# The loop over steps 3 to 6 of a dense convolution block, written out on every engine

## The chip, the cores and the metric

The kernel runs on one core of one Trainium2 chip. The metric is the device time of that core in microseconds (us), as the median of several executions. A profiled execution gives in addition a page and a trace; its span is measured from the first to the last instruction.

## What is computed

Two blocks follow each other on a float32 image batch `x` of 16 x 32 x 32 x 32 (images, channels, rows, columns). The first:

```python
x1 = relu(conv2d(x, w1, b1, 2, 2))
x2 = relu(conv2d(concatenate((x, x1), 1), w2, b2, 2, 2))
x3 = relu(conv2d(concatenate((x, x1, x2), 1), w3, b3, 2, 2))
x4 = relu(conv2d(concatenate((x, x1, x2, x3), 1), w4, b4, 2, 2))
fea = relu(concatenate((x, x1, x2, x3, x4), 1))
fea = einsum('ij,bcjk,lk->bcil', H, fea, H)
out = conv2d(fea, w6, b6, 1, 1) + x
```

Each `conv2d` is a 3x3 convolution; the first four are dilated by 2. The second block quantises its input and its weights to four bits, with one scale for each tensor, and computes

```python
out = relu(_qconv(x, w1))
out = relu(_qconv(out, w2, stride=1, padding=1, groups=PLANES))
out = _qconv(out, w3)
return out + x
```

Since a scale needs the maximum over the whole tensor, the second block starts when the first is done for all images.

## The kernel before

`dense_block` computes the first block, two images (u = 0 and 1) a step. Steps 0 to 7 each convolve one pair; the transform with H and the last convolution ("mix", `stage1`, `stage3`) of a pair lag behind, so that step s also mixes pair s - 1, and step 8 only finishes. Every engine has its own `step(s, odd, batch)`, a hand-written order of work, and all engines run it through `steps` (line 151 and after): 0, 1 and 2 are written out, 3 to 6 stand as a loop of two passes with two steps in each, 7 and 8 are written out. In the loop the step's number is a register, so every wait whose count depends on it (`pe.wait_ge(halo_in[2][u], (s + 1) * 32)` and its like) has the count worked out on the engine's sequencer first, or compares with a register that is counted up.

Engines meet at semaphores alone. What matters below is one step of TensorE (PE), in its order:

- `conv0` and `conv0_on` (line 768), 36 matmuls on x of both images;
- `mix(p, 0)` (lines 871 and 875);
- `conv1_alone` (line 827) and `conv1` (line 768), which end what x2 needs;
- `stage3` of the pair before (line 909), 1.0 us;
- `conv2(s, 0)` and `conv2(s, 1)` (line 768, 9 matmuls each), which read tile `D2`, the split x2, with its halo rows. They wait for `halo_in[2][u]`;
- `mix(p, 1)`, `conv3` (line 827) and `stage1` (line 900).

A halo is made of DMAs that copy 32 partitions of `D` to other partitions of `D`, shifted by a row: `halos` on SyncE (SP), lines 219 and 222, and for `D2` of image 0 one of the two on ScalarE's queue (`halo_2`, line 354). They start when VectorE (DVE) has split x2 (`split_2`, line 490), which follows `conv1_alone` by two additions (lines 499 and 505). So in each step the way from `conv1_alone` over DVE and the DMAs to `conv2` runs beside `conv1` and `stage3` on PE.

SP also issues in each step the loads of x for the next pair (line 212), of x for the mix (229), of the residual (289), and the gathers of the features into `F` (239). The second block, `quantised_block`, has loops of its own on PE, DVE and ACT (lines 1258, 1061, 1070, 1140, 1195).

Of the kernel before, what the change touches and what calls it, by code (L numbers as in the profile page):

```python
# [77 lines left out]
def dense_block(nc, block, semaphore, x_res, x_pads, x_mix, w_conv, bias, w_mix, h_cols, h_rows, b6, w_int, ident_in, keep):  # L78
# [7 lines left out]
    with ExitStack() as ctx:  # L86
# [65 lines left out]
        def steps(eng, step):  # L152
            step(0, 0, -1)
            step(1, 1, 0)
            step(2, 0, 0)
            with eng.Fori(0, 2) as k:
                step(k * 2 + 3, 1, k + 1)
                step(k * 2 + 4, 0, k + 1)
            step(7, 1, 3)
            step(8, 0, 3)  # L160
# [48 lines left out]
        def _(sp):  # L209
# [44 lines left out]
            def step(s, odd, batch):  # L254
# [34 lines left out]
                sp.dma_start(xb[odd][:].rearrange("p u n -> p (u n)"), x_res[s]).then_inc(xb_in[odd], 16)  # L289

            steps(sp, step)

        @block.gpsimd
# [22 lines left out]
        def _(act):  # L316
# [102 lines left out]
            def step(s, odd, batch):  # L419
# [37 lines left out]
                if not is_before_last(s):  # L457
                    copy_4(1)

            steps(act, step)  # L460

            act.wait_ge(sum_done, 2 * PAIRS - 2)
# [9 lines left out]
        def _(dve):  # L472
# [202 lines left out]
            def step(s, odd, batch):  # L675
# [79 lines left out]
                low_4(s, 1)  # L755

            steps(dve, step)

        @block.tensor
# [743 lines left out]
```

## Time and profile before

| what | value |
|---|---|
| median of 3 runs | 394.29 us (392.97 to 395.1) |
| profiled execution, its own time | 394.38 us |
| span of the profiled execution | 392.6 us |
| PE busy | 370.5 us, 94% of the span |
| DVE, ACT busy | 289.0 us, 234.6 us |
| granted TensorE clock, mean | 0.986 |

The profile's page gives busy times of each engine, their course over the span in 40 slices, the DMA queues, the chain of work that ended last and the costliest groups of instructions. PEld is the loading of weights, which overlaps the matmuls.
A row of a stretch gives its bounds and length, the busy time of PE, PEld, DVE, ACT and POOL with their numbers of instructions, the granted clock, the mean share of the DMA engines and GB/s. A row of a timeline gives start, length, engine, line and what was done, and in brackets the idle time before it and what ended it; a row of the chain gives start, length and what. A row of a DMA queue gives its number and kind, packets, MB and share of the stretch on 16 engines; a row of DMA issues gives what was moved by which queue, how often, KB each, and the time from issue to landing.

The trace gives the same for stretches: in the profiled execution step 2 runs on PE from 66.40 to 101.87 us, step 3 to 137.59, step 4 to 174.57, step 5 to 210.05, step 6 to 245.52, and step 7's last stage follows from about 281 us on. The loop's back edge is therefore at 174.57 on PE, its entry at 101.87 and its exit at 245.52.

### The profile page before, as it was taken

The numbers are of one execution on the slowest core, as the hardware profiler recorded it, in microseconds if no ns is written. First come the engines' busy times: TensorE is split into PE (matmuls) and PEld (weight loads), VectorE is DVE, ScalarE is ACT, GpSimd is POOL, SyncE is SP. The second block draws the span as 40 slices with busy tenths as digits, with TensorE's granted clock in tenths as the row PEclk, the third lists the DMA queues.
The fourth block names the chain that finished last, engine by engine and source line by source line (L and its number), as shares of the span: only waits on it lengthen the run. The fifth ranks groups of instructions, "written<-read, shape, count | busy, mean of one in ns | idle before, by whom it ended". The sixth has DMA issues, their size and how long they took to land.

```text
span 392.6 us, 8020 instructions
## 1 busy us (share of the span) xinstructions
PE 370.5 (94%) x2870; PEld 270.8 (69%) x2873; DVE 289.0 (74%) x545; ACT 234.6 (60%) x377; POOL 13.5 (3%) x17
## 2 busy tenths in 40 slices
PE   8989999999999999899999999999984897999986
PEld 7867876878687788668786877887663342455532
DVE  5867678558937984696589379846986699677876
ACT  5446659537743955395367449544846696287761
POOL 6000000300030000000000000000000000000000
PEclk9999999999999999999999999999997699999999
DMA  8847254315333622453253334224100000000004
GB/s 242 237 100 189 66 119 142 93 45 131 100 80 89 173 61 53 100 144 93 48 120 104 79 86 113 60 55 112 55 2 2 1 0 0 3 2 2 4 27 187
DMA packets 19533, 32.56 MB, mean 83 GB/s; under 512 B 4528, under 2 KB 11568, under 8 KB 19504
## 3 DMA queue, kind: packets, MB, share of 16 engines
q1 hardware_dynamic: 18864, 31.14, 30.4%
q10 hardware_dynamic: 640, 1.03, 1.2%
q8 instruction: 18, 0.29, 0.3%
q14 instruction: 11, 0.09, 0.1%
HBM read 11.38 MB, written 2.10 MB: 34 GB/s over the span
## 4 chain that ended last, share of the span: by engine, by line
PE 78%; DVE 11%; DMA 4%; issue 3%; ACT 2%; DVEq 0%; ACTq 0%
PE sums_ps L768 28%; PE mix_ps L871 12%; PE ps L1307 7%; PE mix_ps L900 5%; PE mix_ps L827 5%; PE sums_ps L827 5%; PE mix_ps L875 4%; DMA D<-D 4%; PE ps L1347 3%; PE ps L1274 2%; DVE part L499 2%; PE mix_ps L909 1%; PE ps L1271 1%; PE mix_ps L811 1%; DVE q_I L1190 1%
## 5 line engine op out<-in xcount | busy, mean ns | idle before, releaser
L768 PE MATMUL sums_ps<-D,w_hl 128*128 128x512 f32 x504 | 122.9, 399 | 2.0 <-DMA D<-D 2.0
L768 PEld LDWEIGHTS sums_ps<-D,w_hl 128*128 128x128 f32 x504 | 93.5, 188 | 32.2 <-issue 6.3
L871 PE MATMUL mix_ps<-mix_hl,F_hl 128*128 128x288 f32 x360 | 64.4, 296 | 0.5 <-ACT Y L390 0.5
L390 ACT ACTIVATE Y<-mix_ps 128x288 f32<-128x288 f32 x120 | 48.9, 410 | 24.1 <-PE mix_ps L875 12.2
L871 PEld LDWEIGHTS mix_ps<-mix_hl,F_hl 128*128 128x128 f32 x360 | 55.4, 190 | 2.8 <-ACT Y L390 1.2
L328 ACT ACTIVATE r<-sums_ps,bias_sb 64x512 f32<-64x512 f32 x28 | 19.1, 682 | 48.2 <-PE sums_ps L768 48.1
L499 DVE TENSOR_TENSOR part<-mix_ps,part 64x512 f32<-64x512 f32 x16 | 11.1, 693 | 38.9 <-PE mix_ps L827 38.4
L1073 ACT ACTIVATE q_I<-ps,w_bias 128x1024 f32 x24 | 25.4, 1110 | 16.6 <-PE ps L1307 16.6
L875 PE MATMUL mix_ps<-mix_hl,X 96*128 96x288 f32 x120 | 35.3, 298 | 0.0
L1307 PE MATMUL ps<-q_q,diag 64*64 64x512 bf16 x576 | 33.3, 389 | 0.4 <-DVE q_q L1168 0.4
L348 ACT ACTIVATE D<-part 64x512 fp32r<-64x512 f32 x16 | 10.7, 670 | 32.6 <-DVE part L505 32.6
L1307 PEld LDWEIGHTS ps<-q_q,diag 64*64 64x64 bf16 x576 | 19.2, 105 | 14.5 <-issue 0.9
L900 PE MATMUL mix_ps<-Y,hc 32*32 32x512 f32 (+1 forms) x576 | 24.4, 567 | 0.6 <-ACT Y L390 0.6
L827 PE MATMUL mix_ps<-D,w_hl 128*128 128x512 f32 x96 | 23.9, 397 | 0.0
L827 PE MATMUL sums_ps<-D,w_hl 128*128 128x512 f32 x96 | 23.7, 396 | 0.0
L481 DVE CAST D<-r 64x512 fp32r<-64x512 f32 x32 | 13.4, 419 | 14.0 <-ACT r L328 13.3
L564 DVE SCALAR_TENSOR_TENSOR values<-St,b_sb,xb 64x128 f32<-64x128 f32 (+1 forms) x64 | 22.2, 346 | 0.9
L483 DVE TENSOR_TENSOR D<-r,D 64x512 fp32r<-64x512 f32 x32 | 21.9, 684 | 1.1
L875 PEld LDWEIGHTS mix_ps<-mix_hl,X 96*128 96x128 f32 x120 | 22.5, 189 | 0.0
L531 DVE SCALAR_TENSOR_TENSOR X<-part,X 32x512 fp32r<-32x512 f32 x32 | 21.8, 681 | 0.7
L1274 PE MATMUL ps<-q_xq,w_q 128*128 128x386 bf16 x72 | 21.0, 355 | 0.2 <-ACT q_I L1067 0.2
L522 DVE SCALAR_TENSOR_TENSOR F_hl<-F,F_hl 128x1024 fp32r<-128x1024 f32 x16 | 19.5, 1217 | 2.1 <-ACT F_hl L364 1.8
(133 smaller groups left out, 510.6 us busy)
## 6 DMA issues: line engine op xcount, KB each, us to landing
D<-D SPq DMA_DIRECT2D x88, 126.0 KB, 2.3
x_own<-in_x_pads SPq DMA_DIRECT2D x16, 288.0 KB, 3.7
F<-r SPq DMA_DIRECT2D x64, 64.0 KB, 2.0
F<-in_x_mix SPq DMA_DIRECT2D x16, 128.0 KB, 2.4
F<-part SPq DMA_DIRECT2D x32, 64.0 KB, 2.0
xb<-in_x_res SPq DMA_DIRECT2D x8, 256.0 KB, 2.7
out<-q_res SPq DMA_DIRECT2D x8, 256.0 KB, 2.0
w_raw<-in_w_conv SPq DMA_DIRECT2D x6, 192.0 KB, 4.4
```

The costliest lines, as they stand in the source:

```text
L390: nc.scalar.activation(Y[:, u, g], banks(p, u)[:, g % 4, 0:MIX], ACT.Copy).then_inc(y_out, 1)
L483: nc.vector.tensor_tensor(out=own(f, u, 1), in0=src, in1=high.bitcast(F32), op=ALU.subtract).then_inc(own_ready[u], 1)
L531: last = nc.vector.scalar_tensor_tensor(out=X4[u][low, h], in0=part[u][k].rearrange("p a b l -> p (a b l)"), scalar=0.0, in1=X4[u][k, h].b ...
L564: last = nc.vector.scalar_tensor_tensor(out=keep.values[64 * pi:64 * pi + 64, batch, m, PH // 2 * a:PH // 2 * (a + 1), :], in0=st[k, pi], ...
L768: last = nc.tensor.matmul(conv_sums(s, u)[:, bank, :], w_hl[:, wp, n, d, :], D[f][u][:, xp, :, 4 * d:4 * d + RUN], start=start and d == 0 ...
L827: last = nc.tensor.matmul(side_sums(s, u, f), w_hl[:, w, n, d, :], D[f - 1][u][:, x, :, 4 * d:4 * d + RUN], start=d == 0 and w == 0, stop= ...
L871: nc.tensor.matmul(y, F_hl[u][:, xp, h, k], mix_hl[:, wp], start=n == 0, stop=False, skip_group_check=True)
L875: nc.tensor.matmul(banks(p, u)[:, g % 4, 0:MIX], X4[u][:, g // 4, NP * (g % 4):NP * (g % 4) + NP], mix4_hl[:], start=False, stop=True, ski ...
L900: last = nc.tensor.matmul(out[32 * dy:32 * dy + 32, j, 0:PX // 4 * len(us)], hc[k, d], y, start=d == 0, stop=d == 2, skip_group_check=True)
L1073: nc.scalar.activation(I[:, g, b, 0:PX], ps[:, 2 * b:2 * b + 2].rearrange("p k n -> p (k n)"), ACT.Relu, bias=keep.w2_bias[:, bass.ts(g, 1 ...
L1274: last = nc.tensor.matmul(c1_slot(ps, j)[:, h], w_q[:, bass.ts(k * 2 + par, NP)], x_low[:, at:at + CUT], start=j not in C1_OFFSET, stop=True)
L1307: last = nc.tensor.matmul(ps[64 * col:64 * col + 64, 2 * (two + b) + h], diag[rows, g, at:at + 2].rearrange("p q c -> p (q c)"), field[:, ...
```

## The change

The loop becomes a Python loop that is run when the program is built: each engine's code for steps 3 to 6 then stands twice as long, `s` is a number in all of it, and the functions that ask for it (`is_first`, `no_next` and the like) answer as before. Nothing else is touched. The four loops of the second block stay.

```diff
             step(0, 0, -1)
             step(1, 1, 0)
             step(2, 0, 0)
-            with eng.Fori(0, 2) as k:
+            for k in range(2):
                 step(k * 2 + 3, 1, k + 1)
                 step(k * 2 + 4, 0, k + 1)
             step(7, 1, 3)
```

PE, middle of step 3, from the end of `mix(p, 0)` to the start of `mix(p, 1)`, before (`D` are the convolutions' inputs, `Zt` the transform's):

```order
L875 MATMUL mix_ps<-mix_hl,X 128x288
L833 REGISTER_ALU
L835 ISA
L827 MATMUL mix_ps<-D,w_hl 128x512 x6
L835 REGISTER_ALU
L827 MATMUL mix_ps<-D,w_hl 128x512 x6
L768 MATMUL sums_ps<-D,w_hl 128x512 x18
L968 REGISTER_ALU
L906 ISA
L909 MATMUL mix_ps<-Zt,hr 32x256 x4
L906 REGISTER_ALU
L909 MATMUL mix_ps<-Zt,hr 32x256 x4
```

The same place of the changed kernel:

```order
L875 MATMUL mix_ps<-mix_hl,X 128x288
L827 MATMUL mix_ps<-D,w_hl 128x512 x12
L768 MATMUL sums_ps<-D,w_hl 128x512 x18
L909 MATMUL mix_ps<-Zt,hr 32x256 x8
L768 MATMUL sums_ps<-D,w_hl 128x512 x18
```

The matmuls stand in the same order; the six register instructions between them are gone. Over a pass of two steps PE's waits and register instructions together are 48 before and 20 now (counted in the two built programs).

SP, from the end of step 2 into step 3, before:

```order
L289 DMA xb<-in_x_res 128x512 [waits mx_done]
L156 UNCONDITIONAL_BRANCH
L156 ISA
L212 ISA [waits x_split1,x_split0]
L212 DMA x_own<-in_x_pads 128x576
L212 ISA
L212 DMA x_own<-in_x_pads 128x576
L229 ISA [waits f_lo0]
L229 DMA F<-in_x_mix 32x1024
L236 REGISTER_ALU
L239 DMA F<-r 32x512 [waits relu_done0]
```

and of the changed kernel:

```order
L289 DMA xb<-in_x_res 128x512 [waits mx_done]
L212 DMA x_own<-in_x_pads 128x576 [waits x_split1,x_split0]
L212 DMA x_own<-in_x_pads 128x576
L229 DMA F<-in_x_mix 32x1024 [waits f_lo0]
L239 DMA F<-r 32x512 [waits relu_done0]
```

The transfers and their waits stand in the same order; the registers that held addresses and counts are gone.

## Rows read from the trace of the kernel before

**Rows 1.** The profile's page: span, PE's busy time, chain by engine

```profile
span 392.6 us, 8020 instructions
...
PE 370.5 (94%) x2870; PEld 270.8 (69%) x2873; DVE 289.0 (74%) x545; ACT 234.6 (60%) x377; POOL 13.5 (3%) x17
...
PE 78%; DVE 11%; DMA 4%; issue 3%; ACT 2%; DVEq 0%; ACTq 0%
```

**Rows 2.** Stretches: steps 2 to 6, busy time of each engine

```profile
66.40:101.87 35.47, 35.47 (x249) 28.11 (x249) 25.93 (x46) 21.36 (x39) 3.04 (x3) 1.00 0.39 98
101.87:137.59 35.72, 35.72 (x249) 28.12 (x249) 25.96 (x46) 21.33 (x39) 3.04 (x3) 1.00 0.39 98
137.59:174.57 36.98, 35.56 (x249) 28.20 (x249) 25.87 (x46) 21.33 (x39) 0.95 (x2) 1.00 0.38 95
174.57:210.05 35.48, 35.48 (x250) 28.18 (x249) 25.90 (x46) 21.37 (x39) 0.00 (x0) 1.00 0.38 97
210.05:245.52 35.47, 35.47 (x249) 28.17 (x249) 25.89 (x46) 21.32 (x39) 0.00 (x0) 1.00 0.34 81
```

**Rows 3.** Timeline of PEld at the starts of steps 4 and 5

```profile
137.51 0.53 PEld L768 LDWEIGHTS sums_ps<-D,w_hl 128*128 128x128 f32 x3 [0.84 <-issue]
...
174.50 0.53 PEld L768 LDWEIGHTS sums_ps<-D,w_hl 128*128 128x128 f32 x3 [0.84 <-issue]
```

**Rows 4.** The chain (start, length, what) at `conv2` of steps 3, 4 and 5

```profile
122.74 4.62 PE sums_ps L768 x18
...
154.83 5.00 DMA D<-D
...
195.44 4.39 PE sums_ps L768 x18
```

**Rows 5.** PE's timeline at `conv2` of steps 4 and 7

```profile
159.88 1.66 PE L768 MATMUL sums_ps<-D,w_hl 128*128 128x512 f32 x6 [1.42 <-DMA D<-D]
...
266.58 2.12 PE L768 MATMUL sums_ps<-D,w_hl 128*128 128x512 f32 x8 [0.19 <-DMA D<-D]
```

**Rows 6.** DMA queues: whole span; steps 3; 4; packets of 5 and 6

```profile
q8 instruction: 18, 0.29, 0.3%
...
q8 instruction: 3, 0.05, 0.7%
...
q8 instruction: 2, 0.03, 0.4%
...
DMA packets 3843, 6.32 MB, mean 89 GB/s; under 512 B 897, under 2 KB 2433, under 8 KB 3843
```

**Rows 7.** DMA queues of 86.2:86.3, 121.7:121.9, 157.2:157.3, 263.7:263.8

```profile
q8 instruction: 1, 0.02, 54.9%
...
q8 instruction: 1, 0.02, 32.3%
...
q8 instruction: 1, 0.02, 59.9%
...
q8 instruction: 1, 0.02, 79.2%
```

**Rows 8.** DMA issues at 119.1, 154.8, 191.8, 262.8: halo of image 0

```profile
D<-D ACTq DMA_DIRECT2D x1, 126.0 KB, 3.1
...
D<-D ACTq DMA_DIRECT2D x1, 126.0 KB, 5.0
...
D<-D ACTq DMA_DIRECT2D x1, 126.0 KB, 2.9
...
D<-D ACTq DMA_DIRECT2D x1, 126.0 KB, 3.7
```

**Rows 9.** Timeline of SP: second halo DMA of image 1, steps 3 to 5

```profile
122.17 1.03 SPq L222 DMA_DIRECT2D D<-D  x1
...
157.65 0.89 SPq L222 DMA_DIRECT2D D<-D  x1
...
194.69 0.60 SPq L222 DMA_DIRECT2D D<-D  x1
```

## The prediction

> **What bounds the kernel now.** I read the page first, then the span cut into steps, then what stands at the loop's edges, then the few waits of TensorE (PE) that are left in the loop. On the page PE is busy 94% of 392.6 us and makes 78% of the chain that ended last [rows 1]. Cut into steps, the picture is sharper: in step 2, which is written out, PE is busy for all of its 35.47 us, and in step 6, which is the last quarter of the loop's work, for all of its 35.47 us too; step 5 takes 35.48, step 3 35.72 and step 4 36.98 [rows 2]. DVE and ACT are busy 26 and 21 us of each [rows 2]. So these steps are PE's, back to back, and whatever is done by a sequencer beside them is covered. The one thing to find is why steps 3 and 4 are longer than their twins 5 and 6, which run the same code: 0.25 and 1.50 us. The chain and PE's timeline answer: in step 4 the matmuls of `conv2` wait 1.42 us for the halo of `D2` [rows 5], a DMA issued at 154.83 that took 5.00 us [rows 4]. In step 3 `conv2` is 4.62 us long instead of 4.39 as in step 5 [rows 4], a small wait between its two images. In step 7 the same wait is 0.19 us [rows 5].
>
> The DMA rows then show what those places have in common. The twin halo takes 2.9 us in step 5, 3.1 in step 3, 3.7 in step 7 and 5.0 in step 4 [rows 8]. The engines' code arrives in 16 KB packets (18 of them are 0.29 MB) on an instruction queue, 3 in step 3 and 2 in step 4, while in steps 5 and 6 together all 3843 packets are under 8 KB, so none is of this kind [rows 6]: the second pass finds its code in place. And one of these packets starts at 86.2, 121.7, 157.2 and 263.7 us, which is 19.8, 19.9, 19.6 and 18.2 us into steps 2, 3, 4 and 7 [rows 7], in the middle of the halos that `conv2` waits for. 59.9% of 0.1 us on 16 engines is 0.96 us, the time that this one packet holds one DMA engine; the others come to 0.88, 1.03 and 1.27 us [rows 7]. I take it that a halo is spread over the DMA engines and lands when the slowest is done; then one engine held for 1 us can delay all of it. SP is touched as well: its issue of the last halo DMA takes 0.60 us in step 5, 1.03 and 0.89 in steps 3 and 4 [rows 9].
>
> **Part 1: the branches and the loop register.** Entry, back edge and exit on PE, DVE, ACT and SP go. What they cost is read at PE's back edge, the only place where they could lengthen the step: before the first weight load of step 5, behind the back edge, the loader idles 0.84 us, and before that of step 4, in the middle of the loop's body with no branch, 0.84 us as well [rows 3]. PE works on the last transform's matmuls meanwhile. On DVE and ACT a branch stands in 35 us of which 9 and 14 are idle [rows 2]. Gain: 0. Above, it is bounded by the difference of steps 5 and 2, 0.01 us.
>
> **Part 2: the counts in registers.** 28 instructions of PE's sequencer in two steps go, and more on ACT and DVE. Step 2 has constants everywhere, step 6 registers everywhere; both take 35.47 us, with the same 28.1 us of weight loads and the same DVE and ACT time within 0.05 us [rows 2]. Gain on the path: 0. The cover here is PE's backlog of matmuls; where PE waits for others, as in the way from `conv1_alone` to `conv2`, the register instructions are done before the semaphore arrives. If none of this held, the gain would still be under the 0.01 us just read.
>
> **Part 3: the code gets longer.** This is the one part that can move the time, and it goes both ways. In the built programs PE has 4,763 instructions before and 5,745 after, with matmul and weight load as two and the float32 matmuls of the transform doubled as in the trace. 18 packets for 4,763 are about 260 each, so I take 256 a packet, and 982 more instructions are 4 more packets: two in step 5 and two in step 6, where there is none now. A step is 249 matmuls and 249 loads [rows 2] and, with constants, some 10 waits: about 506 to 508 instructions, 4 to 6 under two packets. So every step has one fetch in its middle and one at its end, and the middle one slips later by that much from step to step; in the loop of before the extra registers (14 a step) made it slip earlier, which is why step 4's comes 0.3 us sooner than step 3's. Between a fetch in step 3 that cost 0.25 us and one in step 4 that cost 1.50 us lie these 0.3 us [rows 2, 7].
>
> Now place them. Half a step's 14 register instructions less puts step 3's fetch some 10 instructions later, step 4's some 23, step 5's and 6's a further 6 each. PE passes 36 instructions (18 matmuls) in 4.4 us of convolution, and 32 in the 1.0 us of `stage3`, which lies just there, so an estimate is 20.1 us into step 3, 20.2 into step 4, 20.3 to 20.5 into step 5, 20.9 into step 6 and 21.9 into step 7, each give or take 0.5. Image 0's halo is issued 17.2 us into a step (154.83 less 137.59) and takes 2.9 undisturbed [rows 4, 8], so it is down at 20.1 and these fetches come too late to hold it: step 4's 1.42 us [rows 5] should go. Image 1's second DMA is issued 20.1 us into step 5 (194.69 less 174.57) [rows 9]; from the same row it is late by 0.3 to 0.4 us if a fetch is under way, and its conv2 half starts 2.2 us after the first, at 23.1. Step 3 is the nearest row for what this is worth: 0.25 us. A fetch deeper in this transfer can cost more; the ends are 0 (step 2's fetch at 19.8 cost nothing, 35.47 us) and 1.5 (step 4's) for each [rows 2, 7]. I take 0.25 for steps 3, 4 and 5 and 0.5 for steps 6 and 7, where the estimate falls deepest into image 1's transfer.
>
> The sum, in waits of PE on the halo: before, 0.25 + 1.50 + 0 + 0 + 0.2 = 1.95 us. After, 0.25 + 0.25 + 0.25 + 0.5 + 0.5 = 1.75. Difference -0.2 us. Against the profiled execution, 394.38 us (span 392.6 and 1.8 around it), this gives 394.2; that execution lies 0.1 above the median of the three runs, 394.29, so I forecast **394.1 us**.
>
> The other engines' code grows too, by one small packet or so each on ACT, DVE and SP; the nearest price is the same wait, and these are half as long. I cost them at nothing and keep up to 0.5 us in the range. The second block's loops stay and only lie at other addresses.
>
> A rule speaks of this change. The Trainium skill, "Runtime: NRT & Kernel Launch", section "Instruction fetch mechanics", says that a taken branch whose target is not in the window of loaded pages stalls for a fetch, and that kernels therefore prefer to be unrolled. The same section gives PE 128 KiB, 2048 instructions, which the body of some 1,040 fits into. By the rule's first half each back edge would be worth a fetch; the trace does not agree, since step 5 starts after the same 0.84 us as step 4 and no packet comes in.
>
> **The rivals.**
>
> *All collisions gone* (faster). If the later fetches miss the halos altogether, as step 2's did, steps 3 to 7 are all 35.47 us and 1.95 us go: 394.3 - 1.95 = 392.4. For it: step 2. Against it: SP's issue of the last halo DMA was slow in both loop steps that had a fetch [rows 9], and the fetches of steps 6 and 7 slip into the transfer.
>
> *The fetches hit two more halos hard* (slower). Steps 5 and 6 have no code fetch now and take 35.48 and 35.47 [rows 2]. If the fetch there falls as unluckily as in step 4, each costs 1.5 us, and if step 4's stays, the time is 394.3 + 3.0 = 397.3. It decides where the fetch starts while more than half of a halo's transfer is still to come. For it: the only fetch that came a little early cost 1.5. Against it: the code's length moves them later, not earlier, and image 1 has more slack, 0.7 us.
>
> *The branch did stall an engine* (faster). If entry and back edge each hid a fetch of about 1 us on DVE or ACT that held up PE later, 2 us would go: 392.3. Against it: no longer step stands behind either edge [rows 2].
>
> *Nothing moves at all* (same): the fetch of step 4 hits as before and steps 5 and 6 get 0.25 each: 394.8.
>
> **How the numbers follow.** Forecast 394.1 with a chance of 0.60; nothing moves, 394.8, 0.17; all gone 392.4, 0.11; hit hard 397.3, 0.09; a hidden stall 392.3, 0.03. About 0.5%, 2.0 us, is what a measurement of this kernel can tell from no change: bounds 392.3 and 396.3. The forecast's own spread is the bounds of five waits of 0 to 1.5 us that hardly all fall one way, 393.0 to 395.6. The range leaves out hard hits and the far side of the clean cases: 392.4 to 396.2. Faster by over 0.5%: half of the clean case and of the stall, 0.07. Slower: 0.09 and a little of the forecast's tail less the milder hits, 0.09. Same: 0.84.
>
> **What would show it.** Right, part 1 and 2: steps 2 and 5 or 6 equal where no halo is late, the loader's 0.84 us unchanged. Part 3: 22 packets of 16 KB instead of 18, two of them in each of steps 5 and 6, the middle one 20 to 21 us in; step 4 at 35.7 us instead of 36.98; PE's waits inside steps 3 to 7 all on `D<-D`; ACT's halo DMA at 2.9 to 3.1 us in step 4. Wrong: a step that is shorter than 35.47 us, which would mean that registers or branches did cost PE time; a wait of over 1 us in step 5 or 6, which is the slower rival; a new wait on something other than a halo.

## The result: 0.7% slower

| kernel | median | executions | profiled span |
|---|---|---|---|
| before | 394.05 us (392.57 to 395.11) | 19 | 392.6 us |
| loop written out | 396.79 us (395.41 to 398.39) | 19 | 394.1 us |

The ratio is 1.0069, with a 95% interval of 1.0055 to 1.0082: a loss of 2.7 us. Here and below, times are medians of several executions, and step lengths and rows come from the one profiled execution of each kernel. The forecast was 394.1 us in a range of 392.4 to 396.2, so the time lies above the range.

The page of the changed kernel, to be laid beside [rows 1, 6]: span, busy time by engine, instruction queue, chain by engine.

```profile
span 394.1 us, 7685 instructions
...
PE 371.2 (94%) x2873; PEld 270.0 (69%) x2873; DVE 288.7 (73%) x545; ACT 234.5 (60%) x377; POOL 13.5 (3%) x17
...
q8 instruction: 22, 0.36, 0.4%
...
PE 73%; DVE 14%; DMA 6%; issue 3%; ACT 2%; SPq 1%; DVEq 0%; ACTq 0%
```

PE is as busy as before, and DVE and ACT too. What changed is the chain: 5% of the span, about 20 us, has gone from PE to DVE, DMA and SP. The instruction queue has the 22 packets that were forecast instead of 18.

The changed kernel cut into steps 2 to 7, as in [rows 2] (bounds and length, then busy times and counts):

```profile
65.51:101.03 35.52, 35.52 (x250) 28.09 (x249) 25.93 (x46) 21.35 (x39) 3.04 (x3) 1.00 0.38 98
101.03:137.65 36.62, 35.74 (x250) 28.09 (x249) 25.90 (x46) 21.36 (x39) 3.04 (x3) 1.00 0.38 96
137.65:174.25 36.60, 35.73 (x249) 28.08 (x249) 25.89 (x46) 21.34 (x39) 0.95 (x2) 1.00 0.37 95
174.25:211.20 36.95, 35.74 (x250) 28.11 (x249) 25.91 (x46) 21.35 (x39) 0.00 (x0) 1.00 0.38 95
211.20:247.41 36.21, 35.74 (x249) 28.11 (x249) 25.90 (x46) 21.36 (x39) 0.00 (x0) 1.00 0.32 80
247.41:282.88 35.47, 35.47 (x249) 28.16 (x249) 24.54 (x44) 20.21 (x37) 0.00 (x0) 1.00 0.33 78
```

Each of the four steps of the old loop is now 0.7 to 1.5 us over the 35.47 us that a step takes when nothing is late. Steps 3 to 6 sum to 146.38 us against 143.65 before [rows 2]: 2.73 us more. Step 7 gives 0.26 back, because its wait is gone, and step 2 loses 0.05, so that steps 2 to 7 are 2.5 us longer, near the 2.7 of the medians. In the two profiled spans only 1.5 us are seen, above all because this execution of the changed kernel reached step 2 0.89 us earlier (65.51 against 66.40). That seems to be a chance of the start, for both kernels run the same code up to there: by their timelines the 18 passes of the first convolution took 4.48 us here and 5.12 before, and the wait for a DMA at 22 us is 1.42 here and 1.61 before.

The chain through the middle of step 5 (start, length, what):

```profile
187.12 1.42 PE mix_ps L827 x6
...
191.57 0.69 DVE part L505
...
192.28 0.67 ACT D L348
...
193.76 0.59 SPq L219
...
194.39 4.18 DMA D<-D
```

It runs from `conv1_alone` over DVE, ACT and SP's issue of image 1's halo into its second DMA, 4.18 us long. PE's timeline at the end of that halo in steps 3 and 5:

```profile
125.06 2.14 PE L768 MATMUL sums_ps<-D,w_hl 128*128 128x512 f32 x8 [0.88 <-DMA D<-D]
...
198.62 0.73 PE L768 MATMUL sums_ps<-D,w_hl 128*128 128x512 f32 x2 [1.21 <-DMA D<-D]
```

The wait stands between the two images of `conv2`, not in front of the first as in step 4 before [rows 5]. And the packets are there: instruction queue from 195.6 to 195.7 us, then the landings of image 1's halo DMAs issued at 194.3 and 231.3, from the list of DMA issues:

```profile
q8 instruction: 1, 0.02, 103.8%
```

```profile
D<-D SPq DMA_DIRECT2D x2, 126.0 KB, 3.3
...
D<-D SPq DMA_DIRECT2D x1, 126.0 KB, 3.4
```

103.8% of 0.1 us on 16 engines is 1.66 us, for which this packet held one DMA engine, beginning 21.4 us into the step. The "x2" is a median over this halo DMA and the one before it, which were issued one behind the other.

How the packet delays the halo stands in the trace too. A halo DMA of 126 KB is 64 packets of 2016 bytes, four for each of 16 engines. The code packet runs until 197.33. The packets that start from 196.8 to 197.3 us, and those that start from 197.31 to 198.11:

```profile
DMA packets 0, 0.00 MB, mean 0 GB/s; under 512 B 0, under 2 KB 0, under 8 KB 0
...
DMA packets 4, 0.01 MB, mean 10 GB/s; under 512 B 0, under 2 KB 4, under 8 KB 4
...
q1 hardware_dynamic: 4, 0.01, 6.6%
```

The other packets of the halo are long done. The last four, one engine's share, start when the code packet ends and run one after another, 0.84 us for the four (6.6% of 0.8 us on 16 engines). The trace doesn't name the engine of a packet; that four are left over, and that they begin at this moment, is what shows that they stood behind the code packet.

### The profile page after: what moved, and what is told of

Its sections match the earlier page's. It is cut to its first block, busy times and chain, and to the rows that moved or that the text cites. A ratio compares the mean times of both kernels' runs of the same rounds, so it can differ in the third digit from the quotient of the medians.

```text
span 394.1 us, 7685 instructions
## 1 busy us (share of the span) xinstructions
PE 371.2 (94%) x2873; PEld 270.0 (69%) x2873; DVE 288.7 (73%) x545; ACT 234.5 (60%) x377; POOL 13.5 (3%) x17
## 3 DMA queue, kind: packets, MB, share of 16 engines
q10 hardware_dynamic: 640, 1.03, 1.2%
## 4 chain that ended last, share of the span: by engine, by line
PE 73%; DVE 14%; DMA 6%; issue 3%; ACT 2%; SPq 1%; DVEq 0%; ACTq 0%
PE sums_ps L768 23%; PE mix_ps L871 12%; PE ps L1307 7%; DMA D<-D 6%; PE mix_ps L900 5%; PE sums_ps L827 5%; PE mix_ps L875 4%; PE mix_ps L827 4%; PE ps L1347 3%; DVE part L499 2%; PE ps L1274 2%; DVE D L490 2%; DVE part L505 2%; PE ps L1271 2%; DVE q_I L1190 1%
## 5 line engine op out<-in xcount | busy, mean ns | idle before, releaser
L1073 ACT ACTIVATE q_I<-ps,w_bias 128x1024 f32 x24 | 25.4, 1110 | 16.6 <-PE ps L1307 16.6
L827 PE MATMUL mix_ps<-D,w_hl 128*128 128x512 f32 x96 | 23.8, 397 | 0.0
L827 PE MATMUL sums_ps<-D,w_hl 128*128 128x512 f32 x96 | 23.7, 396 | 0.0
L564 DVE SCALAR_TENSOR_TENSOR values<-St,b_sb,xb 64x128 f32<-64x128 f32 x64 | 22.1, 346 | 0.9
L483 DVE TENSOR_TENSOR D<-r,D 64x512 fp32r<-64x512 f32 x32 | 21.9, 684 | 1.1
L875 PEld LDWEIGHTS mix_ps<-mix_hl,X 96*128 96x128 f32 x120 | 22.4, 188 | 0.0
L342 ACT ACTIVATE part<-sums_ps,bias_sb 64x512 f32<-64x512 f32 x28 | 19.0, 684 | 4.0 <-DMA F<-part 3.2
```

The lines of the kernel that those rows point to most:

```text
L483: nc.vector.tensor_tensor(out=own(f, u, 1), in0=src, in1=high.bitcast(F32), op=ALU.subtract).then_inc(own_ready[u], 1)
L564: last = nc.vector.scalar_tensor_tensor(out=keep.values[64 * pi:64 * pi + 64, batch, m, PH // 2 * a:PH // 2 * (a + 1), :], in0=st[k, pi], ...
L827: last = nc.tensor.matmul(side_sums(s, u, f), w_hl[:, w, n, d, :], D[f - 1][u][:, x, :, 4 * d:4 * d + RUN], start=d == 0 and w == 0, stop= ...
L875: nc.tensor.matmul(banks(p, u)[:, g % 4, 0:MIX], X4[u][:, g // 4, NP * (g % 4):NP * (g % 4) + NP], mix4_hl[:], start=False, stop=True, ski ...
L1073: nc.scalar.activation(I[:, g, b, 0:PX], ps[:, 2 * b:2 * b + 2].rearrange("p k n -> p (k n)"), ACT.Relu, bias=keep.w2_bias[:, bass.ts(g, 1 ...
```

## The experiments

Theory **A**: the loss comes from where in a step PE's code is fetched, since a 16 KB packet holds one DMA engine and delays the one share of a halo that lies on it. The rivals: **B**, it comes from the constants or the code of the other engines; **C**, a fetch costs about 1 us wherever it falls; **D**, only image 1's halo can be hit; **E**, it comes from a stop of PE's sequencer.

In what follows "fetch at t" is the start of the middle code packet, counted from the start of its step, and "excess" is the length of steps 2 to 7 in the profiled execution over 6 x 35.47 = 212.8 us.

### e1 and e2: which engine's code

e1 has PE's four middle steps written out and leaves the other engines in the loop; e2 has DVE, ACT and SP written out and leaves PE in it.

```diff
-        def steps(eng, step):
+        def steps(eng, step, written_out=False):
...
+            if written_out:
+                for k in range(2):
...
+            else:
+                with eng.Fori(0, 2) as k:
...
-            steps(pe, step)
+            steps(pe, step, True)
```

> TensorE's program alone is written out, the other engines keep their loop. Theory A (TensorE's code comes in by 16 KB packets during the second pass too, and these hold one DMA engine in the middle of image 1's halo of D2): the whole loss is there, 396.6 to 397.0 us, +2.5 to +3 us over the kernel before, 22 packets on queue 8, steps 3 to 6 of 36.2 to 37 us. Rival B (constant waits on ACT, DVE or SP shift who comes when): this kernel is within 0.7 us of the kernel before, 394.0 us.

> ScalarE, VectorE and SyncE are written out, TensorE keeps its loop. Theory A: no loss, 393.5 to 394.5 us; 18 packets on queue 8, step 4 with its wait of about 1.4 us as in the kernel before, steps 5 and 6 at 35.5 us. Rival B: 396.5 us or more.

e1: 397.28 us, ratio to the kernel before 1.0073 (1.0048 to 1.0098), with 22 packets on PE's instruction queue. e2: 393.86 us, ratio 0.9976 (0.9946 to 1.0007), with 18. The ratios are to the kernel before as measured beside each run; that one's median moved between 393.2 and 394.5 us from one group of runs to the next. Steps 3 and 5 of e1, then steps 4 and 5 of e2:

```profile
101.96:138.56 36.60, 35.74 (x250) 28.09 (x249) 25.95 (x46) 21.32 (x39) 3.04 (x3) 1.00 0.38 96
...
175.04:211.58 36.54, 35.73 (x250) 28.11 (x249) 25.88 (x46) 21.32 (x39) 0.00 (x0) 1.00 0.37 95
```

```profile
136.92:173.86 36.94, 35.55 (x249) 28.18 (x249) 25.89 (x46) 21.37 (x39) 0.95 (x2) 1.00 0.38 94
173.86:209.33 35.47, 35.47 (x250) 28.17 (x249) 25.90 (x46) 21.38 (x39) 0.00 (x0) 1.00 0.38 98
```

The loss is in PE's program alone. With DVE, ACT and SP written out the steps are nearly those of the kernel before, its late step 4 included (step 3 is 0.16 us shorter, step 7 0.17 longer). B falls.

### e3 and e4: the same code, 64 instructions further on

```diff
+            for _ in range(64):
+                pe.sem_inc(unused, 1)
             steps(pe, step)
```

> The changed kernel with 64 more sequencer instructions (increments of an unused semaphore) ahead of TensorE's first step, so that every page of its code begins 64 instructions earlier in the work. Nothing else. Theory A: the middle fetch of a step moves from 21.4 us into a step to about 13 to 15 us, before the halo of D2 is issued (17.2), and the waits at conv2 in steps 3 to 6 go: 392.0 to 392.8 us, steps of 35.5 us. Theory C (any fetch during the steps costs about 1 us wherever it falls): unchanged at 396.8 us.

> The kernel before, loops on all engines, with the same 64 extra instructions on TensorE. Theory A: the waits at conv2 in steps 3 and 4 (0.25 and 1.5 us) and 7 (0.2) go: 392.0 to 392.8 us. Theory C, or no part of the fetches: 394.0 us as before.

e3: 400.66 us, ratio 1.0168 (1.0138 to 1.0199). e4: 400.16 us, ratio 1.0157 (1.0127 to 1.0186). Both times miss the expectation by more than 7 us, and yet the steps came out as theory A has them. Steps 3 and 5 of e3, then its first convolution on PE's timeline, then step 4 of e4, then e4's stretch from 9 to 11 us for PE alone:

```profile
110.05:145.52 35.47, 35.47 (x250) 28.16 (x249) 25.90 (x46) 21.37 (x39) 3.04 (x3) 1.00 0.39 99
...
180.99:216.45 35.46, 35.46 (x249) 28.15 (x249) 25.89 (x46) 21.37 (x39) 0.00 (x0) 1.00 0.39 99
```

```profile
11.30 6.99 PE L812 MATMUL mix_ps<-D,w_hl 128*128 128x512 f32 x18 [6.18 <-issue]
```

```profile
144.22:179.69 35.47, 35.47 (x249) 28.16 (x249) 25.89 (x46) 21.33 (x39) 0.95 (x2) 1.00 0.40 99
```

```profile
9.00:11.00 2.00, 0.00 (x0) 0.50 0.85 264
```

Every one of steps 2 to 7 is 35.46 to 35.48 us in both, excess 0.0, with the fetches of steps 3 and 4 at 13.3 to 13.7 and none later than 17.2. The loss is a price of the edit itself: the increments stand in the trace of e3 from 1.40 to 11.04 us, one each 0.15 us, so the first convolution starts at 11.30 us instead of 4.88. PE has then been idle for 6 us, and the convolution is slower as well: 6.99 us in e3 and 5.88 in e4, where the kernels without padding take 4.48 (changed) and 5.12 (before). In e4 the granted clock is 0.50, the lower of its two levels, from 9 to 11 us; e3's records have it at 1.00 there, although its passes are slower still, so what slowed e3 stays open. Theory C is gone, since fetches at 13 to 17 us cost nothing, but a late start could still be blamed for the even steps, so the padding had to be made cheaper.

### e5 to e8: padding by splitting the warm-up

```diff
-            for _ in range(8):
-                nc.tensor.matmul(mix_ps[:, 3, 0:NP], ones[:], ones[:], start=True, stop=True)
+            for _ in range(16):
+                nc.tensor.matmul(mix_ps[:, 3, 0:64], ones[:], ones[:, 0:64], start=True, stop=True)
```

e5 has this in the kernel before, e7 in the changed one; e8 has 24 of 42 columns, e6 has 2 of 512 (24 instructions less), both in the changed kernel.

> The kernel before, with its 8 warm-up matmuls of 128 columns made 16 of 64: the same columns ahead of the first convolution, 32 more instructions on TensorE. Theory A: the middle fetch moves from 19.8 to 20.1 us into a step to about 16 or 17, ahead of the halos of D2, and that of step 7 from 18.4 to about 15; all steps 2 to 7 at 35.5 us, and nothing is lost at the start: 392.2 to 392.9 us, 1.5 to 2 us under the kernel before. Theory C (the padded kernels' even steps were due to their late start, not to where the fetches fall): 394.0 us, a wait of about 1.4 us in step 4.

> The changed kernel, with its 8 warm-up matmuls of 128 columns made 2 of 512: the same columns, 24 instructions less. Theory A: the middle fetch moves later, from 21.0 to 21.7 us into steps 3 to 6 to about 23 to 25, behind the last halo of D2, as in step 7 of the changed kernel (24.0, no wait): the 4.5 us of waits go, 392.0 to 393.0 us. Theory C: 396.8 us. If the fetch falls upon image 1's halo of D3 or the gathers instead, a wait appears at line 827, and the time lies between.

> The changed kernel with 16 warm-up matmuls of 64 columns, 32 more instructions. Theory A: the middle fetch moves from 21.0 to 21.7 us into a step to about 17.5 to 18.5, where the fetch of step 7 in the kernel before lay (18.4, wait of 0.2 us): image 0's halo is hit at its start, so waits of 0.1 to 1.4 us in each of steps 3 to 6, 393 to 396 us. Theory C: 396.8 us.

> The changed kernel with 24 warm-up matmuls of 42 columns, 64 more instructions, about as many columns. Theory A: the fetches lie as in e3, 13.6 to 17.4 us into the steps, steps 2 to 7 at 35.5 us, but without e3's late start (first convolution at 5 to 7 us instead of 11.3): 392.2 to 394 us. Theory C: 396.8 us or more.

| | median | ratio (95%) | fetch in steps 3 / 4 / 5 / 6 / 7 | excess |
|---|---|---|---|---|
| e5 | 398.69 | 1.0131 (1.0108 to 1.0153) | 16.6 / 18.5 / none / none / 16.6 | 0.4 |
| e6 | 395.72 | 1.0050 (1.0035 to 1.0066) | 23.8 / 23.7 / 23.7 / 24.0 / 23.8 | 1.0 |
| e7 | 397.93 | 1.0122 (1.0101 to 1.0143) | 16.7 / 17.1 / 17.9 / 19.9 / 19.9 | 0.2 |
| e8 | 399.78 | 1.0159 (1.0135 to 1.0182) | 13.5 / 13.6 / 14.4 / 16.7 / 16.6 | 0.0 |

Again no kernel met its expected time. The steps did in e6 (3 to 6) and e8. In e5, step 4 kept 0.39 us, with its fetch at 18.5 instead of the expected 16 to 17. In e7 a wait was expected in each of steps 3 to 6, with fetches at 17.5 to 18.5; they came earlier in steps 3 and 4 and later in step 6, and only steps 6 and 7 lost anything, 0.12 us each. PE's timeline of e5 at the warm-up, and its step 4; then steps 2 and 3 of e6; then step 6 of e7; then step 5 of e8:

```profile
1.34 7.09 PE L987 MATMUL mix_ps<-ones 128*128 128x64 f32 x32 [1.34 <-DVE ones L660]
```

```profile
142.48:178.34 35.86, 35.57 (x250) 28.19 (x249) 25.91 (x46) 21.22 (x39) 0.95 (x2) 1.00 0.39 97
```

```profile
68.15:104.64 36.49, 35.72 (x250) 28.10 (x249) 25.93 (x46) 21.37 (x39) 3.05 (x3) 1.00 0.37 96
104.64:140.11 35.47, 35.47 (x250) 28.17 (x249) 25.89 (x46) 21.39 (x39) 3.05 (x3) 1.00 0.39 99
```

```profile
213.66:249.25 35.59, 35.59 (x250) 28.11 (x249) 25.91 (x46) 21.35 (x39) 0.00 (x0) 1.00 0.34 81
```

```profile
181.47:216.94 35.47, 35.47 (x249) 28.16 (x249) 25.90 (x46) 21.39 (x39) 0.00 (x0) 1.00 0.39 98
```

Halving the columns did not halve the warm-up's time: 32 passes of 64 columns took 7.09 us, 0.22 us each, where 16 of 128 took 3.78. So e5, e7 and e8 start 3.3 us and more late, and their first convolution takes 5.49 to 6.59 us as well, at a granted clock of 1.00; why is open. e6 starts on time, though its first convolution takes 5.45, and is the cleanest of these: with the fetch behind the last halo, at 23.7 and later, steps 3 to 6 lose all of their 4.5 us; but step 2, whose fetch moved from 19.9 to 21.4, is now 36.49, and step 1 lost some 1.4 us in the same way. Moving all pages by one amount moves the damage to other steps.

### e9 to e11: padding that costs nothing

```diff
                     for h, (wp, xp) in enumerate(((0, 0), (0, 1), (1, 0))):
+                        if more:
+                            pe.sem_inc(unused, 1)
                         last = nc.tensor.matmul(conv_sums(s, u)[:, bank, :], ...
```

`more` is set in convolutions of x in steps 1 and 2: 54 increments, one ahead of each of 54 matmuls, in the kernel before (e9) and in the changed one (e10); e11 has the 18 of step 1 alone, in the changed one.

> The kernel before, loops kept, with 54 increments of an unused semaphore in TensorE's program, one ahead of each of 54 convolution matmuls of steps 1 and 2: one takes the sequencer 0.15 us (e3's trace) and a matmul 0.24, so they should cost no time. Theory A: the middle fetches of steps 2 to 4 and 7 move to about 13 to 16 us into the step, all steps 2 to 7 take 35.5 us: 392.0 to 392.6 us, 1.5 to 2 us under the kernel before. If the extra instructions are not covered: up to 54 x 0.15 = 8 us more.

> The changed kernel with the same 54 instructions. Theory A: its fetches lie at 14 to 18 us into steps 3 to 7, no or nearly no waits at conv2, and the time is that of e9 within 0.5 us (392.0 to 393.0): then all of the changed kernel's loss is where its code is fetched, and branches and registers are worth nothing. If it stays 1 us or more above e9, something else in the written-out loop costs time; if it is 1 us or more below, the loop did cost time.

> The changed kernel with 18 such instructions, in step 1 alone. Theory A: the middle fetch moves from 21.0 to 21.7 us into steps 3 to 6 to about 19 to 20, into image 0's halo, as step 4's in the kernel before: waits of 0.2 to 1.5 us in front of conv2's first image in steps 3 to 6 instead of between the two images, 395 to 398 us. Theory D (only the halo of image 1 can be hit): 392.5 us.

e9: 392.01 us, ratio 0.9974 (0.9951 to 0.9996). e10: 391.66 us, ratio 0.9969 (0.9943 to 0.9995). e11: 394.65 us, ratio 1.0028 (1.0005 to 1.0050). Steps 4 and 5 of e9, then of e10:

```profile
137.24:172.72 35.48, 35.48 (x250) 28.17 (x249) 25.90 (x46) 21.32 (x39) 0.95 (x2) 1.00 0.40 98
172.72:208.19 35.47, 35.47 (x249) 28.16 (x249) 25.89 (x46) 21.45 (x39) 0.00 (x0) 1.00 0.39 98
```

```profile
137.20:172.67 35.47, 35.47 (x249) 28.17 (x249) 25.89 (x46) 21.34 (x39) 0.95 (x2) 1.00 0.39 98
172.67:208.14 35.47, 35.47 (x249) 28.16 (x249) 25.91 (x46) 21.34 (x39) 0.00 (x0) 1.00 0.39 99
```

Both have no excess, both start on time, and they differ by 0.35 us in the median, with intervals that cover each other. This is the comparison that prices the change as such: with the fetches out of the way, a loop and the same steps written out take the same time, steps 2 to 7 being 212.84 us in both profiles and the intervals of both ratios reaching about 1 us to either side. By the medians, the changed kernel lies 2.7 us above the kernel before and e10 1.5 below it, 4.3 in all, where the changed kernel's steps have an excess of 4.5. Both are also the best versions found, some 1.2 us (e9) and 1.5 us (e10) under the kernel before as measured beside them (393.18), whose profile has an excess of 2.0 us to give back. e10's time is 0.3 us under what was expected of it.

e11 was to move the fetches into image 0's halo. Steps 4 to 7, with the fetches at 19.9, 19.9, 20.7 and 21.4:

```profile
136.55:172.06 35.51, 35.51 (x249) 28.10 (x249) 25.89 (x46) 21.37 (x39) 0.95 (x2) 1.00 0.38 98
172.06:208.34 36.28, 35.73 (x249) 28.10 (x249) 25.91 (x46) 21.38 (x39) 0.00 (x0) 1.00 0.38 96
208.34:244.41 36.07, 35.73 (x249) 28.11 (x249) 25.90 (x46) 21.38 (x39) 0.00 (x0) 1.00 0.33 80
244.41:281.13 36.72, 35.73 (x249) 28.10 (x249) 24.57 (x44) 20.24 (x37) 0.00 (x0) 1.00 0.32 75
```

Excess 2.7, but not where it was expected: no step waits for image 0. Its last halo packet is down at 19.9 us here, as in a step without a fetch, so a fetch at 19.9 is too late for it, and the waits of steps 5 to 7 all stand between the two images. In step 5:

```profile
195.76 2.36 PE L772 MATMUL sums_ps<-D,w_hl 128*128 128x512 f32 x9 [0.55 <-DMA D<-D]
```

Theory A's place for these waits was wrong, and theory D's was right for this kernel, though not its time (392.5); that image 0 can be hit stands in [rows 5], step 4. The time fell short of the expected 395 by 0.35. Step 7, free of any wait in the changed kernel with its fetch at 23.8, now has the longest one.

### e12: a packet of no use

e9, and in steps 5, 6 and 7 a copy of 16 KB from HBM to HBM on GpSimd's queue, released together with image 1's halo:

```diff
+            for n, s in enumerate((5, 6, 7)):
+                pool.wait_ge(own_ready[1], s * 3 + 2)
+                pool.dma_start(aside[:, 0:4093], x_mix[0:1, 0:4, :].rearrange("b c n -> b (c n)")[:, 0:4093]).then_inc(aside_in, 16)
+                pool.wait_ge(aside_in, 16 * (n + 1))
```

> e9 (loops kept, fetches out of the way, steps 2 to 7 at 35.5 us) and, in steps 5, 6 and 7, one more copy that nobody in the kernel needs: 16 KB of x in HBM to other HBM, issued on GpSimd's queue as one piece of 4093 elements when the halo of D2 of image 1 is released (19.5 us into the step). It imitates a fetch packet and crosses no page of TensorE's code. Theory A (a DMA engine that is held for about 1 us in the middle of a halo is enough): if the copy is on one engine and starts 20.5 to 21.7 us into the step, conv2 waits 0.5 to 1.5 us in each of the three steps, 393.5 to 396 us. Rival E (only the fetch of TensorE's own code costs time, by stopping its sequencer): steps 5 to 7 stay at 35.5 us, 392.0 us. If the copy is spread over the engines or comes after 22.5 us, both expect 392.0 and nothing is told apart.

Steps 4 to 7; then its queue from 193.35 to 193.45 us; then the queue of the halo from 194.64 to 194.95; then the chain in step 5:

```profile
136.45:171.92 35.47, 35.47 (x250) 28.16 (x249) 25.89 (x46) 21.35 (x39) 0.95 (x2) 1.00 0.39 99
171.92:207.91 35.99, 35.72 (x250) 28.09 (x249) 25.89 (x46) 21.34 (x39) 0.71 (x1) 1.00 0.37 96
207.91:243.83 35.92, 35.73 (x250) 28.11 (x249) 25.89 (x46) 21.37 (x39) 0.53 (x1) 1.00 0.33 80
243.83:279.96 36.13, 35.71 (x249) 28.10 (x249) 24.49 (x44) 20.24 (x37) 0.52 (x1) 1.00 0.32 77
```

```profile
q0 software_dynamic: 12, 0.02, 83.1%
```

```profile
q1 hardware_dynamic: 4, 0.01, 6.6%
```

```profile
192.03 3.26 DMA D<-D
```

Nearly all of the copy is one packet of 16,372 bytes. It starts 21.5 us into the step and holds one engine for about 1.3 us (83.1% of 0.1 us on 16), until 194.64. Again the last four packets of the halo start when it ends. Steps 5, 6 and 7 grow by 0.52, 0.45 and 0.66 us, 1.6 together, and the wait is on `D<-D`; step 4, without a copy, stays. The median is 393.95 us, ratio 0.9993 (0.9974 to 1.0012), against e9's 0.9974: by ratios about 0.7 us, less than the profile's 1.6 and inside what two intervals of this width allow. The kernel before had 394.43 us beside this run and 393.18 beside e9, so the median of e12 alone would decide nothing; the steps do. A large packet in the middle of the halo is enough; PE's own code and its sequencer are not needed for a wait, and rival E, that only a stop of the sequencer costs time, falls. The same copy at a harmless place of the step was not run.

The real packets cost more than these copies at equal length (1.01 to 1.13 us in four steps with packets of 1.21 to 1.28 us, against 0.52 for a copy of 1.25). The traces show most of the difference in the four packets left over: they take 0.8 to 0.9 us behind a code packet and 0.33 behind the copy (6.6% of 0.31 us on 16). Why they are slower there is open. What PE waits for is then only how late the halo ends:

| packet in step | its length | last packet of image 1's halo ends, us into the step | cost |
|---|---|---|---|
| none, or away from the halos | | 22.1 to 22.3 | 0 |
| copy, e12, 6 and 7 | 1.19, 1.35 | 22.96, 23.18 | 0.45, 0.66 |
| code, changed kernel, 6 | 0.96 | 23.15 | 0.74 |
| code, changed kernel, 4 | 1.21 | 23.46 | 1.13 |
| code, changed kernel, 5 | 1.66 | 23.87 | 1.48 |

In sixteen steps of all the traces this end comes later than 22.7. In fifteen of them, those of e12 included, the cost is that end less 22.4, within 0.13 us; step 5 of e11 has 0.23 more. A stop of PE's sequencer could add little to that.

## Why the prediction was wrong, point by point

**What bounds the kernel.** Right. PE back to back at 35.47 us a step, its only waits in steps 3 to 7 on halos, and the code packets as their cause: e3, e4, e9 and e10 have 35.46 to 35.48 in every step once the packets are elsewhere, and e12 makes the wait without them. That a halo lands when its slowest share does, which the prediction took as given, is what the four packets left over show.

**Part 1, branches, and part 2, registers: 0.** Right. The idle time of the weight loader at the start of step 5 is still 0.84 us:

```profile
174.18 1.46 PEld L768 LDWEIGHTS sums_ps<-D,w_hl 128*128 128x128 f32 x7 [0.84 <-issue]
```

and e9 against e10 gives the two parts together as nothing in the steps of the profiles, and as 0.35 us in the medians, which intervals of about 1 us on either side don't tell from zero. The Trainium skill's page "Runtime: NRT & Kernel Launch" (section "Instruction fetch mechanics") names the stall behind a taken branch as one reason to unroll; this case's traces show none at the back edge, where the loader idles 0.84 us with the loop [rows 3] and without it. The same section calls the crossing of a 16 KiB boundary "mostly hidden"; here such crossings cost 4.5 us in four steps of the changed kernel.

**Part 3, four more packets.** The number is right (22), their place and price are not, and this is the step that failed.

- *Place.* The prediction said "20.1 us into step 3, 20.2 into step 4, 20.3 to 20.5 into step 5, 20.9 into step 6 and 21.9 into step 7, each give or take 0.5". Measured: 20.8, 21.4, 21.4, 21.4 and 23.8. I moved the fetches at PE's pace by so many instructions. They don't glide.
- *Price.* Step 3 of the kernel before (0.25 us at 19.9) was taken as "the nearest row". It was the nearest in time, and not in kind: there the packet is nearly over when image 1's packets start, and only SP's issue is late [rows 9]. At 21.4 it is in the middle of them, and one engine's share of the halo comes behind it. The slack of 0.7 us was too large as well: it is 0.3 to 0.4, for the last halo packet ends at 22.1 undisturbed, and the cost begins when it ends later than about 22.4 to 22.5. Priced 0.25 + 0.25 + 0.25 + 0.5 = 1.25 for steps 3 to 6, measured 1.15 + 1.13 + 1.48 + 0.74 = 4.50; step 7, priced 0.5, cost nothing. The waits of before were summed rightly, 1.95 against 2.0.
- *The bound was there.* Part 3 gives the ends as 0 and 1.5 for each step. With 1.5 for each of steps 3 to 6 the sum is 392.4 + 6.0 = 398.4; the range stopped at 396.2, on the ground that the waits "hardly all fall one way". They did: the four steps run the same code, so one mistake in placing was made in all four at once.

The other engines' code was put at nothing, rightly as far as e2 shows, which has it written out and is no slower than the kernel before. The second instruction queue brings 11 packets of 8 KB within the span in the kernel before, in the changed one, in e1 and in e2 alike; the one more for each engine that the prediction counted on did not come.

**The rivals.** "The fetches hit two more halos hard", 397.3 us at a chance of 0.09, is the one that came nearest. Its kind of mechanism was right, its closeness in time is luck: it has step 4's wait for image 0 stay and two more like it, 4.5 us, where four steps wait for image 1, 4.5 us. It was argued down with image 1's slack, and argued for with step 4's as "the only fetch that came a little early", though step 7's, at 18.2, came earlier still and cost 0.26. Step 4's wait in front of image 0 did go, as forecast (ACT's halo is no longer in the chain there); its place was taken by one behind it. "All collisions gone" was possible, as e10 shows, but not with these pages.

What each fetch cost, from all kernels, as length of its step over 35.47:

| fetch, us into the step | cost, us |
|---|---|
| 13.3 to 18.2 | 0 |
| 18.2 to 18.5 (step 7 of the kernel before, steps 7 and 4 of e2, step 4 of e5) | 0.26, 0.43, 1.47, 0.39 |
| 19.6 (step 4 before) | 1.51 |
| 19.8 to 19.9 | 0, 0, 0.02, 0.04, 0.05, 0.09, 0.12, 0.12, 0.25, 0.81 |
| 20.7 to 21.5 | 0.60, 0.74, 0.76, 1.01, 1.02, 1.07, 1.13, 1.13, 1.15, 1.25, 1.48 |
| 23.7 and later | 0 |

Within a row the cost goes with the length of the packet. At 19.8 to 19.9, packets of 0.88 us cost 0 to 0.04, those of 0.93 to 0.96 us 0.02 to 0.12, and those of 1.03 and 1.31 us 0.25 and 0.81. At 21.3 to 21.5, 0.96 us cost 0.74 and 0.76, 1.21 to 1.28 us 1.01 to 1.13, 1.44 us 1.25 and 1.66 us 1.48. Why one packet lasts longer than another, and why step 4 of the kernel before lost 1.51 us to one of 0.96 us, is open; there the last four packets of ACT's halo ended 1.1 us later than the code packet.

## What to carry to other kernels

Writing a loop out does not only remove branches; it adds code, and here this code came in through the same DMA engines as the data, a packet of 16 KB at a time, at places that moved with the number of instructions ahead of them. Where PE waits for DMAs with less than about 1 us to spare (a packet lasted 0.9 to 1.7 us here), look for the instruction queue in the stretch of each such wait, and compare repetitions of the same step: if one is late and its twin is not, an edit that only shifts pages may win or lose more than the edit it comes with. To judge such an edit, measure it with and without some idle instructions placed where another engine's or PE's own backlog covers them; and when a term is the same for several repetitions, take it at its worst in all of them for the range.

## What was not expected of the hardware

- The start of code fetches clusters at a few places of a step (most often 19.9, 21.4, 23.8 us in steps of 35.5) instead of moving evenly with the number of instructions ahead.
- A 16 KB code packet holds one DMA engine for 0.88 us at 86.2 us of the kernel before and for 1.66 us in the middle of a halo's packets (step 5 of the changed kernel). The share of the halo on that engine, four packets, waits for its end, and behind a code packet these four took 0.84 us, behind a copy of the same size 0.33.
- One increment of a semaphore in PE's program takes its sequencer 0.15 us: 64 in a row held back the first convolution from 4.88 to 11.30 us, but 54 of them, one ahead of each of 54 matmuls of 0.24 us, cost nothing that can be seen.
- At the start of the kernel a float32 pass of 64 columns took 0.22 us and one of 128 columns 0.24: fewer columns did not make it shorter.
